# Splitting gate weights beside causal attention: one shared output buffer, and the conversion moved two to three masked groups later

## The reference

```python
x = x + _L0_attn_ref(_layernorm(x), Wq, Wk, Wv)        # causal attention, 16 heads of 16
x = x + _L0_ffn_ref(_layernorm(x), Wg, bg, Wu, bu, Wd, ...)
# in _L0_ffn_ref: mlp = silu(h @ Wg + bg) * (h @ Wu + bu) @ Wd + bd;  Wg, Wu are 256 x 1024
```

## Time and profile before

| | |
|---|---|
| time, 3 runs | 4314.35 us median (4313.3 to 4316.14) |
| time of the profiled execution | 4314.35 us |
| its span, first to last instruction | 4312.6 us |
| mean granted PE clock | 0.978 |
| busy: PE, PEld, DVE, ACT, POOL | 94%, 55%, 65%, 62%, 36% |
| attention | from the start to about 1285 us |

### The profile page before, as it was taken

The page is one execution under the profiler, slowest core; times in us unless marked ns, Lnnn a source line. Parts: engine busy times, 40 slices in busy tenths (PEclk is TensorE's granted clock), DMA queues, the critical chain, the costliest instruction groups (busy, mean ns, idle before and its releaser), DMA issues. The chain is left out here.

```text
span 4312.6 us, 65428 instructions
## 1 busy us (share of the span) xinstructions
PE 4047.0 (94%) x23476; PEld 2363.6 (55%) x23476; DVE 2816.3 (65%) x5635; ACT 2658.4 (62%) x3262; POOL 1553.8 (36%) x1303
## 2 busy tenths in 40 slices
PE   7999999999986999999999989997999999999999
PEld 4445444444535787887878765554344444444443
DVE  6777777777747878787887845444554554554553
ACT  2555555555566545455554524443888888888888
POOL 3122122222224535344444411110445445445445
PEclk7999999999998999999999999998999999999999
DMA  7334333433403242323323220002676676676673
GB/s 176 94 96 96 90 87 80 111 81 89 103 25 114 59 117 60 104 73 91 86 78 99 72 65 1 1 1 54 152 164 156 141 164 155 141 164 155 141 164 91
DMA packets 205761, 429.96 MB, mean 100 GB/s; under 512 B 47585, under 2 KB 72561, under 8 KB 189057
## 3 DMA queue, kind: packets, MB, share of 16 engines
q1 hardware_dynamic: 193360, 411.56, 39.6%
q0 software_dynamic: 4160, 6.35, 0.6%
q10 hardware_dynamic: 7920, 7.87, 0.6%
HBM read 338.59 MB, written 87.03 MB: 99 GB/s over the span
## 5 line engine op out<-in xcount | busy, mean ns | idle before, releaser
L2240 ACT ACTIVATE gelu_out<-hidden,b_col 128x1024 f32<-128x1024 f32 x1024 | 1084.4, 1112 | 163.0 <-PE hidden L2140 162.3
L2222 POOL TENSOR_TENSOR combined<-combined,gated 128x512 f32<-128x512 f32 x480 | 619.6, 1291 | 663.7 <-DVE gated L2337 455.1
L705 DVE TENSOR_REDUCE maxima<-front 128x1 f32<-128x512 f32 (+3 forms) x1280 | 737.7, 631 | 172.4 <-PE front L513 98.8
L605 ACT ACTIVATE probsT<-scoresT 128x1024 f32<-128x1024 f32 (+3 forms) x768 | 585.5, 811 | 297.8 <-PE scoresT L541 294.2
L1169 POOL TENSOR_TENSOR pair_sums<-sims 128x1024 f32<-128x1024 f32 x256 | 483.3, 1905 | 665.9 <-DVEq L1301 412.3
L2337 DVE SCALAR_TENSOR_TENSOR gated<-expert_out,b_col,gates_spread 128x512 f32<-128x512 f32 x480 | 360.1, 750 | 502.0 <-PE expert_out L2150 296.2
L2140 PE MATMUL hidden<-slice_stack,w_stack 128*128 128x512 f32 x2048 | 627.0, 428 | 15.0 <-ACT gelu_out L2240 15.0
L2150 PE MATMUL expert_out<-gelu_out,w_sb 128*32 128x512 f32 x4096 | 548.2, 607 | 24.4 <-DVE gated L2337 13.5
L2140 PEld LDWEIGHTS hidden<-slice_stack,w_stack 128*128 128x128 f32 x2048 | 352.0, 189 | 371.0 <-ACT gelu_out L2240 282.2
L1097 PE MATMUL dense<-xnT,dense_weights 128*128 128x512 f32 x2304 | 536.3, 394 | 13.7 <-ACT silu_down L1203 9.3
L450 POOL TENSOR_SCALAR_AFFINE_SELECT probsT<-probsT 128x512 f32<-128x512 f32 x256 | 167.0, 655 | 957.8 <-ACT probsT L605 956.3
(11 more groups left out here) (205 smaller groups left out, 5164.0 us busy)
## 6 DMA issues: line engine op xcount, KB each, us to landing
gates_spread<-gate_scratch SPq DMA_DIRECT2D x512, 256.0 KB, 4.9
dense_weights<-dense_scratch SPq DMA_DIRECT2D x384, 256.0 KB, 2.9
stack_scratch<-split_parts SPq DMA_DIRECT2D x192, 256.0 KB, 3.1
slice_stack<-slice_scratch SPq DMA_DIRECT2D x128, 256.0 KB, 7.9
q_stack<-stack_scratch SPq DMA_DIRECT2D x64, 384.0 KB, 6.2
k_stack<-stack_scratch SPq DMA_DIRECT2D x64, 384.0 KB, 9.3
slice_scratch<-slice_parts SPq DMA_DIRECT2D x32, 512.0 KB, 6.3
out_x<-x_tiles ACTq DMA_DIRECT2D x15, 512.0 KB, 5.0
```

Source lines behind the costliest of these rows:

```text
L605: nc.scalar.activation(PT[:, i % NPT, 2 * pr:2 * pr + 2, at:BANK], ST[pr][:, :, at:BANK], ACT.Exp, scale=SCALE).then_inc(probs_ready, 1)
L705: nc.vector.tensor_reduce(dst, F[k % 3][:, 0:parts * w].rearrange("p (a k) -> p a k", a=parts), AX.X, ALU.max)\
L2222: nc.gpsimd.tensor_tensor(CM[:, par, hc, :], CM[:, par, hc, :], Y[:, u % 2, :], ALU.add)\
L2240: nc.scalar.activation(GH[:, k % 4, :, :], HP[k % HPB][:, :, :], ACT.Gelu, bias=b1c[:, u % E:u % E + 1])\
```

## The change

The raw pieces get a buffer of their own with two slots (`RAW`), and the two parts of a piece go to one single buffer (`PARTS`). SBUF in use stays the same, 1024 bytes a partition. Waits follow from that: the load of piece k waits until the low part of piece k-2 has been made; the high part of piece k, on ACT, waits in addition until piece k-1 is stored. The high part moves from masked group 4k+4 to 4k+6 and the low part with its store from 4k+4 to 4k+7. With that, high parts fall on groups 10, 14, 22 and 2 (the last in the step that follows), and low parts on groups 11, 15, 23 and 3. The loads stay where they are. The last two pieces are placed at masked groups 254 and 255.

```diff
     def load_piece(self, pool, raw, k):
-        wait(pool, self.stored[k % 2], 16 * (k // 2))
-        pool.dma_start(parts[:, k % 2, 1, :].bitcast(F32), ...)
+        wait(pool, self.low_made, k - 1)
+        pool.dma_start(raw[:, k % 2, :], ...)
             .then_inc(self.raw_in[k % 2], 16)

     def high_part(self, act, raw, parts, k):
         act.wait_ge(self.raw_in[k % 2], 16 * (k // 2 + 1))
-        self.nc.scalar.activation(parts[:, k % 2, 0, :], parts[:, k % 2, 1, :].bitcast(F32), ACT.Copy)
+        wait(act, self.stored, 16 * k)
+        self.nc.scalar.activation(parts[:, 0, :], raw[:, k % 2, :], ACT.Copy).then_inc(self.high_made, 1)

     def low_part(self, pool, raw, parts, k):
         pool.wait_ge(self.high_made, k + 1)
-        self.nc.gpsimd.tensor_tensor(parts[:, k % 2, 1, :], parts[:, k % 2, 1, :].bitcast(F32),
-                                     parts[:, k % 2, 0, :].bitcast(F32), ALU.subtract)
+        self.nc.gpsimd.tensor_tensor(parts[:, 1, :], raw[:, k % 2, :], parts[:, 0, :].bitcast(F32), ALU.subtract)
         pool.wait_ge(self.low_made, k + 1)
-        pool.dma_start(self.scratch[...], parts[:, k % 2, :, :].bitcast(F32)).then_inc(self.stored[k % 2], 16)
+        pool.dma_start(self.scratch[...], parts[:, :, :].bitcast(F32)).then_inc(self.stored, 16)

-        PARTS = sb("dense_pieces", [P, 2, 2, dense.COLS], F32R)
+        RAW = sb("dense_raw", [P, 2, dense.COLS])
+        PARTS = sb("dense_pieces", [P, 2, dense.COLS], F32R)
         LOAD_AT = {EVERY * k: k for k in range(NPC)}
-        HIGH_AT = {MASKED[min(EVERY * k + 4, len(MASKED) - 1)]: k for k in range(NPC)}
-        LOW_AT = {min(EVERY * k + 4, len(MASKED) - 1): k for k in range(NPC)}
+        HIGH_AT = {MASKED[min(EVERY * k + 6, len(MASKED) - 2 + k // (NPC - 1))]: k for k in range(NPC)}
+        LOW_AT = {min(EVERY * k + 7, len(MASKED) - 2 + k // (NPC - 1)): k for k in range(NPC)}

     # SP, before the next layer reads the stored parts
-                    for i in range(2):
-                        sp.wait_ge(dense_w.stored[i], 16 * len(dense_w.pieces) // 2)
+                    sp.wait_ge(dense_w.stored, 16 * len(dense_w.pieces))
```

More of the change, by code:

```diff
@@ L110, in __init__, with load_piece, high_part, low_part @@
         self.low_made = ctx.enter_context(nc.semaphore("dense_low_made"))
-        self.stored = [ctx.enter_context(nc.semaphore(f"dense_stored{i}")) for i in range(2)]
+        self.stored = ctx.enter_context(nc.semaphore("dense_stored"))
         self.down_stored = ctx.enter_context(nc.semaphore("down_stored"))
-    def load_piece(self, pool, parts, k):
+    def load_piece(self, pool, raw, k):
         i, f, c, h = self.pieces[k]
-        wait(pool, self.stored[k % 2], 16 * (k // 2))
-        pool.dma_start(parts[:, k % 2, 1, :].bitcast(F32),
-                       self.weights[i][c * P:(c + 1) * P, f * P + h * self.COLS:f * P + (h + 1) * self.COLS])\
+        wait(pool, self.low_made, k - 1)
+        pool.dma_start(raw[:, k % 2, :], self.weights[i][c * P:(c + 1) * P, f * P + h * self.COLS:f * P + (h + 1) * self.COLS])\
             .then_inc(self.raw_in[k % 2], 16)
-    def high_part(self, act, parts, k):
+    def high_part(self, act, raw, parts, k):
         act.wait_ge(self.raw_in[k % 2], 16 * (k // 2 + 1))
-        self.nc.scalar.activation(parts[:, k % 2, 0, :], parts[:, k % 2, 1, :].bitcast(F32), ACT.Copy)\
-            .then_inc(self.high_made, 1)
-    def low_part(self, pool, parts, k):
+        wait(act, self.stored, 16 * k)
+        self.nc.scalar.activation(parts[:, 0, :], raw[:, k % 2, :], ACT.Copy).then_inc(self.high_made, 1)
+    def low_part(self, pool, raw, parts, k):
         i, f, c, h = self.pieces[k]
         pool.wait_ge(self.high_made, k + 1)
-        self.nc.gpsimd.tensor_tensor(parts[:, k % 2, 1, :], parts[:, k % 2, 1, :].bitcast(F32),
-                                     parts[:, k % 2, 0, :].bitcast(F32), ALU.subtract).then_inc(self.low_made, 1)
+        self.nc.gpsimd.tensor_tensor(parts[:, 1, :], raw[:, k % 2, :], parts[:, 0, :].bitcast(F32), ALU.subtract)\
+            .then_inc(self.low_made, 1)
         pool.wait_ge(self.low_made, k + 1)
         pool.dma_start(self.scratch[self.DOWN + 2 * f + i, :, :, c, h * self.COLS:(h + 1) * self.COLS],
-                       parts[:, k % 2, :, :].bitcast(F32)).then_inc(self.stored[k % 2], 16)
+                       parts[:, :, :].bitcast(F32)).then_inc(self.stored, 16)
 def causal_attention(nc, x, X, STATS, MEAN, RS, B, Wq, Wk, Wv, ident, dense):
@@ L452, in _ @@
                 if k in LOW_AT:
-                    dense.low_part(pool, PARTS, LOW_AT[k])
+                    dense.low_part(pool, RAW, PARTS, LOW_AT[k])
                 if k in LOAD_AT:
-                    dense.load_piece(pool, PARTS, LOAD_AT[k])
+                    dense.load_piece(pool, RAW, LOAD_AT[k])
         @block.tensor
@@ L607, in exponential @@
                 if pr == 1 and i in HIGH_AT:
-                    dense.high_part(act, PARTS, HIGH_AT[i])
+                    dense.high_part(act, RAW, PARTS, HIGH_AT[i])
                 if pr == 1 and kt == 1 and i >= NG // 6:
```

## The result

| | before | after |
|---|---|---|
| median | 4315.25 us (4 runs, 4313.3 to 4319.51) | 4370.1 us (4 runs, 4364.87 to 4375.27) |
| ratio | | 1.0124, 95% interval 1.0105 to 1.0142 |
| profiled execution, its span | 4314.35, 4312.6 us | 4367.08, 4365.3 us |
| mean granted PE clock | 0.978 | 0.970 |

I had forecast 4346 with a range from 4326 to 4366. The direction and the place were right; the size was not. The waits between 180 and 1330 us show the mechanism (us in total, times, longest), first of the changed kernel, then of the kernel before.

What follows compares the result with a forecast made beforehand. The prediction took PE to bound the attention, busy 960 of 1000 us. Pauses 17.5, clock 8.6 and 4.3, and end 1.1 sum to 31.5 us, which added to 4314.35 gives 4346, range 4326 to 4366.

Steps and rivals of the forecast that it cites:

- pauses, 14 places: At starts of steps 1 to 14, PE loses 1.65 us in seven odd and 0.85 in seven even steps: 17.5 us.
- end of the attention: At the attention's end, ACT waits once for a store with nothing queued; the last output copy starts 1.1 us later.
- Buffers, load's wait, moved POOL work at nothing: Throughout the attention, same instructions, a load's wait that costs nothing, and POOL work moved within each quartet: 0 us.
- The place of the stall: ACT waits for stores at group 2 of steps 1 to 14, about 4.2 us each, and once at the end.
- The landing, 9.2 us after the issue: Group 23's store, issued 1.84 us after the first stack load, lands 11.0 us after that load.
- One row of step 0: The store of 177.56, behind four stack loads, took 8.0 us, landing 11.0 us after the first; taken for the landing.
- the upper bound: Group 23's store lands 11.9 us after the first stack load, from the load of 89.75; adds 12.6 us in all.
- the others 2 to 4: Expected sign: stores behind group 23's mask take 9 to 10 us to land, all other stores 2 to 4.
- No part made up later: In the attention, PE recovers none of its pauses afterwards, as it bounds; for the low end a third, 5.8 us.
- The clock, 1.23 us a fall: After PE's pauses, the lower clock costs 1.23 us each: 8.6 us for seven odd steps, 4.3 for half the even.
- The range's upper end: 4366 us; its rival, landing at 11.9 with 14 clock falls (17.2 us), adds 48.4 us: 4363; no separate chance given.
- The rule on round robin: DMA engines alternate between queue rows by packet, so stores pass the stack loads; only the end is late: 4315.5 us.

Runs made afterwards that it cites:

- e1: Changed kernel with two high-part slots and one low, the wait for the previous piece's store moved from ACT to POOL: 4320.06 us, 1.0007 to the kernel before.
- e2: Changed kernel with its new buffers and wait, but high and low parts back at masked group 4k+4: 4316.5 us, 0.9996 to the kernel before.
- e7: Kernel before with eight needless PE transposes added at each of the same 14 places, where it has no pause: 4334.59 us, 1.0037 to the kernel before.
- e4: Changed kernel with SP issuing the step-end stack loads only after group 23's store has landed: 4319.93 us, 1.0002 to the kernel before.
- e5: Changed kernel with eight needless PE transposes put ahead of each of its 14 pauses: 4342.32 us, 1.0056 to the kernel before.
- e6: Kernel before with old buffers and waits, only high part moved to masked group 4k+6 and low part to 4k+7: 4361.21 us, 1.0102 to the kernel before.
- e3: Changed kernel with the high part one masked group later, at 4k+7: 4332.17 us, 1.0033 to the kernel before.
- e8: Changed kernel with the high part one masked group earlier, at 4k+5: 4431.41 us, 1.0261 to the kernel before.

## Why the prediction was wrong in size

In its own order, by the profiled executions (4367.08 - 4314.35 = 52.7 us):

| term | predicted | measured |
|---|---|---|
| pauses, 14 places | 17.5 | 23.0 |
| clock | 12.9 | 25.7 (the rest) |
| end of the attention | 1.1 | 1.2 |
| before the first wait | 0 | 2.8 |

- *Buffers, load's wait, moved POOL work at nothing.* Right: e1 and e2 agree with the kernel before within their intervals.
- *The place of the stall, 14 starts of steps and once at the end.* Right. ACT waited 15 times and nowhere else.
- *The landing, 9.2 us after the issue.* Nearly right. 9.4 us in step 3; ACT's wait was 4.6 us in the mean instead of 4.2, and 6.0 and 6.3 in steps 2 and 5. One row of step 0 stood for all; the upper bound was the better guide. The row that gave this bound was no clean one, though. The prediction reads the load of 89.75 as standing behind four stack loads. SP's timeline shows a second four going out with it and three loads of x right after:

```profile
89.75 0.90 SPq L376 DMA_DIRECT2D q_stack<-stack_scratch  x2
90.70 0.91 SPq L376 DMA_DIRECT2D k_stack<-stack_scratch  x2
91.64 17.00 SPq L345 DMA_DIRECT2D x_tiles<-in_L_attn_x  x3
```

That its landing 11.9 us after the first stack load was near what came (1.84 + 9.5 = 11.3 in the mean) is in part luck. The sign "the others 2 to 4" was wrong too, for the seven stores at group 15. PE's pauses grew by 13.0 us in odd steps (predicted 7 x 1.65 = 11.6) and 10.0 us in even ones (7 x 0.85 = 6.0). The even ones are small differences between a landing and a fixed moment, so a few tenths on the landing weigh most there.

- *No part made up later.* Right: step 9 is longer by its pause, and e7's turns are paid in full.
- *The clock, 1.23 us a fall.* This is the step that failed. The term of 12.9 us is 10.5 falls of 1.23 us. The number was nearly right, with ten falls in the 14 places, though not its parts: a fall came behind four of the seven odd pauses and six of the seven even ones, where the term has seven and half of seven. The price was not. I took it from the one fall of step 3 of the kernel before, where the lower clock lasted some 3 us, and gave every fall that size. In step 7 of the changed kernel it lasted 10 us and cost 4.33. The kernel before had a longer fall too, in step 4, that I did not price:

```profile
444.00:454.00 10.00, 9.75 (x54) 3.63 (x50) 4.89 (x8) 4.36 (x8) 3.44 (x6) 0.66 0.04 11
516.00:526.00 10.00, 10.00 (x55) 4.29 (x54) 6.33 (x11) 4.68 (x7) 2.81 (x5) 0.84 0.04 11
```

These are the stretches behind its falls in steps 4 and 5. Both steps were run elsewhere without a fall and with the same wait of PE ahead: step 5 in e1, step 4 in e2. Here are step 5 of the kernel before and of e1, then step 4 of the kernel before and of e2.

```profile
491.72:567.03 75.31, 72.47 (x582) 36.12 (x586) 57.97 (x115) 41.83 (x63) 16.38 (x28) 0.98 0.41 92
492.54:566.77 74.23, 71.34 (x582) 35.61 (x586) 57.90 (x115) 41.92 (x63) 16.40 (x28) 1.00 0.41 93
```

```profile
410.71:491.72 81.01, 76.05 (x598) 37.55 (x602) 61.52 (x123) 44.96 (x71) 16.37 (x28) 0.96 0.36 85
410.69:489.09 78.40, 73.22 (x598) 36.78 (x602) 61.54 (x123) 44.98 (x71) 16.38 (x28) 1.00 0.39 88
```

So a fall cost 1.08 us where the lower clock lasted some 3 us, 2.61 where it lasted 7, and 4.33 where it lasted 10. 1.23 is sound for the short ones alone. I had also no reason to think that a fall after a pause of 1.65 us is like one after 1.35 us of waiting for DVE at another place in the step. The range's upper end carried the mistake on, since it multiplied 1.23 by 14.

- *The rule on round robin* (the Trainium skill, DMA: Bandwidth & Descriptors, section "Queues, rings and completion order"). It would have left the time as it was. For these transfers, POOL's stores behind SP's stack loads, it does not describe what is seen: 9.4 us behind them, 2.0 us ahead of them (e4). Which part of the DMA path keeps the order, the transfer itself or the write of the semaphore, isn't settled by these runs.

The 2.8 us before the first wait: step 0 ends at 188.36 instead of 185.57 (first stack load). Its mean clock between 84 and 140 us is 0.70 against 0.79. In the other kernels it lies anywhere from 0.60 (e5, e6) to 0.79 (e2, e3), and e3, which has the changed kernel's buffers and wait, ends step 0 at 185.94. So I take it for the state of the clock in that early stretch and not for an effect of the change; this is argued, not shown. The 25.7 us are what is left after the other terms. An estimate from the three prices above comes near: the ten falls, three of some 3 us, three of 7 and four of 10, make 28.4 us, the short fall in step 5 that both kernels have stays, and the kernel before's falls in steps 3 and 4 (1.08 and 2.61) are no longer paid beside them, which leaves 24.7. e5 gives 28 us for much the same quantity in another way.

What stays open is when the clock falls, and for how long. The length of the pause alone doesn't decide it. In step 5 PE waited 1.35 us for DVE in the kernel before and 1.34 in e1, at the same place; the first was followed by a fall and the second was not. In the changed kernel 1.16 and 1.26 us were followed by one, 1.47 was not, and in e5 not even 1.75.

## What to carry to other kernels

A wait is priced by what stands behind it in the waiting engine's order, and by what stands ahead of the awaited DMA at its issue. Before adding one, list the bulk loads issued just ahead; the same single buffer was free where the copy came some 22 us behind the store (e2), and cost 0.33%, 1.2% and 2.6% where it came four, three and two masked groups behind one that stood behind the bulk loads (e3, the changed kernel, e8). If it can't be moved, let an engine with room wait (e1), or let the small store go ahead of the large loads (e4). A pause of the bounding PE may cost much more than its length where the clock falls after it, and a fall is to be priced by how long the lower clock lasts, from several falls and not from one.

## What the hardware showed that I had not expected

- A fall of PE's clock after a pause of 1.66 us cost 4.33 us, 2.6 times the pause. Falls came behind pauses as short as 1.16 us, and the lower clock lasted from 3 to 10 us.
- Eight needless transposes ahead of each of 14 pauses made the kernel 28 us faster (4370.1 to 4342.3), by keeping the granted clock at 1.00 instead of 0.96.
- A 64 KB store on POOL's queue, behind four stack loads on SP's, took 9.4 us (8.5 to 11.2 at the 14 places); ahead of them it took 2.0 us.
